# A graph kernel's scatter stage: SyncE asks for a pair's edge attributes one pair earlier

## What is computed

```python
# layer 2 (third): two propagations, weights from the degrees
deg = segment_sum(ones, r); w = dinv[r] * dinv[c]
for _ in range(2):
    x = segment_sum(w[:, None] * x[c], r)

# layer 3 (fourth)
gate = silu(edge_attr @ W1.T + b1) @ W2.T + b2 + adapt_logit   # edge_attr: 206250 x 40
msg = gate * h[dst] * (cw * mj)[:, None]
agg = segment_sum(msg, src)
```

## Time and profile before

| | before |
|---|---|
| runs, us | 6416.88, 6427.56, 6429.94 |
| the profiled execution, us | 6438.38 |
| its span, us | 6436.4 |
| TensorE's granted clock, mean | 0.628 |
| PE busy, us | 3747.3 (58%) |
| DVE busy, us | 4031.9 (63%) |
| ACT busy, us | 2396.8 (37%) |
| POOL busy, us | 4009.8 (62%) |

### The profile page before, as it was taken

The page is one execution under the profiler, slowest core; times in us unless marked ns, Lnnn a source line. Parts: engine busy times, 40 slices in busy tenths (PEclk is TensorE's granted clock), DMA queues, the critical chain, the costliest instruction groups (busy, mean ns, idle before and its releaser), DMA issues.

```text
span 6436.4 us, 120599 instructions
## 1 busy us (share of the span) xinstructions
PE 3747.3 (58%) x46034; PEld 3072.5 (48%) x46035; DVE 4031.9 (63%) x7214; ACT 2396.8 (37%) x5124; POOL 4009.8 (62%) x4023
## 2 busy tenths in 40 slices
PE   8255555454555555434555565555565565898885
PEld 7244444332333333223544455445454455887775
DVE  5443444455555555635667666776676766888999
ACT  2111111111111111113444444444444445788886
POOL 3766666666666666675555665566666665436996
PEclk7555555555555555555666665666666567999998
DMA  4545422222222222212333333333333333687775
GB/s 161 177 156 161 131 49 48 47 57 46 49 48 47 48 49 50 42 33 54 61 60 65 62 62 61 62 64 65 60 63 63 63 63 71 190 231 196 212 213 141
DMA packets 1135498, 576.24 MB, mean 90 GB/s; under 512 B 752611, under 2 KB 1074543, under 8 KB 1134785
## 3 DMA queue, kind: packets, MB, share of 16 engines
q1 hardware_dynamic: 1030017, 457.40, 29.9%
q0 software_dynamic: 104896, 110.96, 7.9%
HBM read 399.84 MB, written 168.16 MB: 88 GB/s over the span
## 4 chain that ended last, share of the span: by engine, by line
another core or an unknown queue 23%; PE 20%; issue 19%; DVE 15%; ACT 10%; POOL 10%; SPq 3%; DMA 1%; DVEq 0%; ACTq 0%; POOLq 0%
PE ps L1388 4%; ACT rb L1772 3%; PE ps L1616 3%; DVE ps L2309 2%; POOL meta_b L1184 2%; POOL meta_b L1181 2%; PE ps L1427 2%; ACT rb L1817 2%; ACT at_table L1817 2%; PE ps L1348 1%; PE ps L1376 1%; DVE row_src L2440 1%; ACT meta_a L1698 1%; DVE row_src L2439 1%
## 5 line engine op out<-in xcount | busy, mean ns | idle before, releaser
L1058 POOL DMA_INDIRECT by_src<-meta_a,row_src x1612 | 1626.6, 1009 | 1055.0 <-issue 475.5
L1046 POOL DMA_INDIRECT ring<-h_table,meta_b x1616 | 1646.9, 1019 | 915.5 <-issue 450.2
L1683 ACT ACTIVATE ring<-ring,meta_b 128x48 f32<-128x48 f32 x1616 | 386.3, 322 | 2141.9 <-DMA ring<-h_table,meta_b 2096.1
L1388 PE MATMUL ps<-ring,WX 128*128 128x48 bf16 x2188 | 439.5, 236 | 537.5 <-DVE row_src L2440 336.3
L1427 PE MATMUL ps<-meta_a,w1T 104*112 104x256 f32 x806 | 428.0, 627 | 501.4 <-DMA meta_a<-in_attrT 225.5
L2804 DVE TENSOR_TENSOR meta_b<-big,ps 128x1152 bf16<-128x1152 bf16 (+1 forms) x546 | 698.7, 1280 | 0.0
L1570 PE MATMUL ps<-dst_i,meta_b 128*128 128x128 bf16 x2450 | 362.1, 285 | 536.6 <-ACT rb L1817 214.6
L1388 PE MATMUL ps<-row_src,WX 128*128 128x48 bf16 x4376 | 499.1, 234 | 272.7 <-issue 271.6
L1388 PEld LDWEIGHTS ps<-ring,WX 128*128 128x128 bf16 x2188 | 359.8, 164 | 558.7 <-DVE row_src L2440 347.5
L1522 PE MATMUL ps<-WX,meta_b 128*128 128x49 bf16 (+1 forms) x14742 | 575.1, 197 | 56.1 <-issue 42.1
L1388 PEld LDWEIGHTS ps<-row_src,WX 128*128 128x128 bf16 x4376 | 440.1, 166 | 314.2 <-issue 312.9
(11 more groups left out here) (388 smaller groups left out, 9012.7 us busy)
## 6 DMA issues: line engine op xcount, KB each, us to landing
by_src<-default SPq DMA_DIRECT2D x44, 1456.0 KB
meta_a<-by_src SPq DMA_DIRECT2D x229, 234.0 KB, 3.8
rb<-lo_rows SPq DMA_DIRECT2D x202, 256.0 KB
rb<-src_rows SPq DMA_DIRECT2D x273, 144.0 KB
rb<-dst_rows SPq DMA_DIRECT2D x273, 144.0 KB
meta_a<-in_attrT SPq DMA_DIRECT2D x402, 80.0 KB
ring<-h_table,meta_b POOLq DMA_INDIRECT x1616
by_src<-meta_a,row_src POOLq DMA_INDIRECT x1612
```

The source lines that it names most:

```text
L1046: pool.indirect_dma_start(ring[:, gg % RING, j, 0:width], None, table, bass.IndirectOffsetOnAxis(ap=index(g * GROUP + j), axis=0)) \
L1058: pool.indirect_dma_start(by_src, bass.IndirectOffsetOnAxis(ap=row_src[:, t:t + 1], axis=0), rec[:, q % RECS, j, :], None).then_inc(s_sc[q ...
L1388: mm = pe.matmul(acc_of(FROM[T] + h, FEAT), hot_w[:, g % 2, h, :, j], rows, start=False, stop=False, skip_group_check=True)
L1683: scaled = act.activation(row, row, ACT.Copy, scale=meta_b[:, t, M_NORM:M_NORM + 1])
```

## The change

Place 0 loads pairs 0 and 1. Every other even place q loads pair q/2 + 1 instead of pair q/2. So the load of pair c stands at place 2c-2 instead of 2c, ahead of everything else of that place. The two waits in front of it keep their values, and the number of loads stays 202.

```diff
--- before.py
+++ after.py
@@ -929,8 +929,10 @@
 
             early_loads = 0
             for q in range(PLACES):
-                if q < QUADS_IN and q % 2 == 0:
-                    c, n = q // 2, min(2, QUADS_IN - q)
+                for c in ([0, 1] if q == 0 else [q // 2 + 1] if q % 2 == 0 else []):
+                    n = min(2, QUADS_IN - 2 * c)
+                    if n <= 0:
+                        continue
                     if c >= 2:
                         sp.wait_ge(s_sp, 2 * (c - 1))
                         sp.wait_ge(s_attr[c % 2], 32 * (c // 2))
```

## The result

The changed kernel takes 6354.83 us, the median of 4 runs (6348.79 to 6362.47), beside 6422.22 for the kernel before (4 runs). The ratio is 0.9903, with a 95% interval from 0.9878 to 0.9927: 62 us less, 47 to 78. The forecast was 95 us less, the range 6222 to 6410. The profiled execution took 6360.09 us (span 6358.2), 78.3 less than that of before.

A forecast was written before the change was run, and what follows sets the result against it. In the scatter stage no engine is full; POOL's 2047 us of batches plus 516 us of gaps make the time. Shorter even gaps, 81 + 14 = 95 us, take the median from 6427.6 to 6333 us; range 6222 to 6410.

The forecast's parts named there:

- step 1: SP's attribute loads: asked for about 13 us sooner, so all 76 waits of PE's HIDDEN should go.
- step 2: POOL's gaps before even batches with an attention step in their own place: 81 and 14 us less, 95 in sum.
- the floor: POOL's gap from PE's late reports: about 1 us to the report, 0.7 to POOL's start; regular odd batches 1.65 us.
- The even batches without a step: POOL's 64 gaps before even batches in places without an attention step, 0.80 us each; left out of the sum.
- The odd batches: POOL's batches whose GATE follows no HIDDEN needing a new pair; 1.34 us gaps with steps in both places, no change summed.
- rival A: POOL's gaps: every even batch becomes like the mean odd one, 196 us less, 6232 us; chance 0.14.
- step 3: SP's queue: the wait for HIDDEN moves one pair earlier; cost taken as 0, bounds nothing to 250 us.
- B: Absorbed: PE's HIDDEN and GATE run earlier but are reported after POOL's batch; 23 us less, 6405 us; chance 0.16.
- C: Nothing: SP's moved wait lets loads out hardly earlier, or gaps reopen in odd batches; 6427 us; chance 0.10.
- D: Slower: PE runs ahead, TAKE's report stays out for two batches; 58 us slower at 30 places, 6486 us; chance 0.10.
- its sign: For rival D: PE's COUNT waits for ACT lengthen; DVE's "remote" wait before needing TAKE was not to grow; no size given.

The follow-up runs named there:

- half-way kernel: Changed kernel with only even-numbered pairs loaded early, odd-numbered at their old place: 6395.71 us beside 6419.15 before (0.9963) on a slower chip; 1.0006 and 1.0007 on quicker ones.
- the pair with one DMA a batch: Kernel before and changed kernel, each with one of four indirect DMAs a batch, slower chip: 5702.55 and 5642.98 us, beside 6343.34 for the full kernel before.
- the variants: Changed kernel with loads one place ahead, only even-numbered pairs early, or no loads after pairs 0 and 1: 1.0003 to 1.0007 of before on quicker chips.

## Why the prediction was right, and what was off

*What the move takes away* (step 1). Right: no wait for the attributes is left. The load is asked for 9.6 us sooner on average (14.3 against 4.7), not 13, and that is enough. The rest is SP's wait for HIDDEN, below.

*What is on the path* (step 2), the even gaps with a step. 81 and 14 us were forecast, 76 and 26 measured. The means came to 1.72 and 1.41 where 1.65 and 1.7 were said. The regular odd batch as the floor of the first class holds. (Of the 33 other odd ones of that class 16 are near nothing, not most.)

*The even batches without a step.* Left out, since a later batch pays for a shorter gap there. They gave 13 us, and the odd ones without a step in their own place took 18. So the reason was right, and it holds for the other even batches too, where it was not applied.

*The odd batches.* This is the term that was mis-sized. It stood in the sum as 0 and is +48 us: 18, 12 and 18. The prediction had the reason in its hands, twice. Besides the place just named, against rival A it said that many odd batches have no gap because the even one before them had a long one in which PE caught up; then it let the even gaps fall and left the odd ones where they were. The half-way kernel shows the link: odd gaps of 0.83 us behind a late pair, 1.08 behind an early one, in one execution. So does the pair with one DMA a batch: -220 and +164 us. With that term the sum is 81 + 14 - 48, or 47 us; with the measured even ones it is 76 + 26 + 13 - 48 = 67, and the stage lost 70. It is partly luck that 95 was no further off: two terms too small by 12 and 13 us made up for half of the missing 48.

*What it could cost* (step 3). 0 was taken and it was next to nothing: DVE waited once for the fields, 2.9 us just behind the stage, at 5357.54, where it had not before. ACT's two longer waits for the index rows, also behind the stage, were there before (11.0 us, now 12.0). But the reason given, that the stores have already made SP wait past that HIDDEN, is not what the trace shows. SP's waits from 3000 to 5300, one row of before and two of after:

```profile
SPq L938 <- PE ps L1427: 0.4, 2, 0.2
```

```profile
SPq L940 <- PE ps L1429: 165.0, 45, 9.7
...
SPq L940 <- remote: 89.2, 28, 7.0
```

SP now stands some 254 us, in 73 times, for HIDDEN to free the buffer. It stands as much less for ACT in front of the stores: 591.5 us before, 332.5 after. The wait has moved, and nothing that mattered stood behind it. That is luck of this queue more than a step of the forecast.

*The rivals.* A fell with the odd gaps: even and odd became alike, but between the two, not at the old odd mean. B's 23 us is under the interval of 47 to 78. C is half true, since the gaps did partly reopen in the odd batches; it took 48 of 115 us. D would have ended slower and did not come, though COUNT's waits for ACT did lengthen (362 to 444.5 us), as its sign was to be. DVE's "remote" waits for TAKE's sums did not (436.9 us before, 418.2 after). D's mechanism is real all the same: the run without POOL's wait for GATE is a kernel in which batches start sooner and hold back GATE's report more often, and it is slower by some 110 us.

*What the prediction could not know.* It rests on the floor, and the floor exists on some chips only. On the quicker ones the change gives nothing (1.0005 and, in the variants, 1.0003 to 1.0007) since POOL has no gaps to shorten. The late reports themselves were named as unexplained. Now it is shown that they come with POOL's batches of four indirect DMAs: with one DMA a batch they are gone on the same chip. What in such a chip holds PE's reports back is open. It was not tried to move TAKE out of the batches.

## What to carry to other kernels

Where an engine's idle time alternates between long and short gaps, the short ones are often short only because of the long ones. Take the mean over the pair, before and after, and not the long class alone. And don't count a late transfer by its waits. Those for this load were 153 us in the half-way kernel and cost nothing under a full POOL; they were 226 us and worth 62 under a POOL with gaps, 247 us and worth 60 with most of POOL's work gone.

## What the runs showed of the hardware

The same program takes 14 to 15% less time on some chips than on others of the same kind: 5448 to 5459 us on two of them, 6343 to 6422 on the others. Of the 905 us between the profiled executions of the changed kernel, all but 10 lie in two stages in which POOL issues indirect DMAs back to back: the 1616 loads ahead of the scatter stage (2538.5 us against 2106.6) and the scatter stage (2583.3 against 2119.7).

On the slower chips PE's reports come late there: TAKE's 3.6 us after its last matmul (median), 0.23 on the quicker ones. When they come out depends on where POOL's batch stands. In the slower trace of the changed kernel 88 TAKEs have their last matmul start 2.0 to 2.5 us into a batch; 81 of them are late, at the median 1.0 us behind the batch's end. All 33 that fall 3.5 to 5 us in are late, at the median 6.7 us behind it, 29 of them behind the end of the next batch. Of the 51 in the first half microsecond 35 are late, but most of these come out within the batch, as in the timeline above. It looks as if a pause of POOL lets the reports out and a start soon after the last end shuts them in again, but that is a reading, and the last group doesn't fit it. DVE's and ACT's reports that the trace has are prompt on the slower chips too; but it has only 54% and 63% of them in the scatter stage, and nearly all on a quicker one, so it says nothing about the rest.

With four DMAs a batch TensorE's granted clock is 0.63 in the slower chips' profiled executions and 0.66 to 0.67 in the quicker ones'. It doesn't explain the difference. In the stage ahead of the scatter stage it is 0.50 on both kinds (600 to 2700 us and 600 to 2260 us), and with one DMA a batch it is 0.66 on a slower chip. A pacing wait that looks superfluous (POOL's for GATE) is worth some 110 us on a slower chip.
